# A two-layer graph network: 64 of the rows that an iteration of the second layer gathers are fetched one by one by the sync engine

## The reference

```
edge_index = stack([src, dst])
h = maximum(layernorm(x), 0)
x = x + layer0(h, node_vec1, src, dst, edge_attr_4, edge_attr_64, ...)
h = maximum(layernorm(x), 0)
x = x + layer1(h, edge_attr_4, W1..W5, Ws, Wv, edge_index)

# layer1
s, v = x[:, :64], x[:, 64:].reshape(n, 32, 3)
ss, vv = s[src], v[src]                       # one row of 160 per edge
...                                            # products with the 4 edge numbers and W1..W5
m_agg = segment_sum(m, dst, num_segments=n)
return x + relu(linear(m_agg))
```

## Time and profile before

| what | us |
|---|---|
| median of 3 runs (2083.0 to 2085.46) | 2085.17 |
| the profiled execution | 2084.44 |
| its span, first to last instruction | 2082.6 |
| first layer's edge loop, about | 55 to 1035 |
| second layer's edge loop, about | 1083 to 2070 |
| busy in the span: PE / DVE / POOL / ACT | 1714.7 / 1276.2 / 1467.8 / 172.3 |

### The profile page before, as it was taken

The page is one execution under the profiler, slowest core; times in us unless marked ns, Lnnn a source line. Parts: engine busy times, 40 slices in busy tenths (PEclk is TensorE's granted clock), DMA queues, the critical chain, the costliest instruction groups (busy, mean ns, idle before and its releaser), DMA issues. The chain is left out here.

```text
span 2082.6 us, 41902 instructions
## 1 busy us (share of the span) xinstructions
PE 1714.7 (82%) x15596; PEld 1466.5 (70%) x15596; DVE 1276.2 (61%) x2725; ACT 172.3 (8%) x391; POOL 1467.8 (70%) x1559
## 2 busy tenths in 40 slices
PE   6889899989899898999737878787878787878786
PEld 4666676767666676767527878787878787878776
DVE  5777878787878787787763444444444444444444
ACT  4100000001010101000140000000000000000000
POOL 1777777777777777777457777777777777777772
PEclk9999999999999999999859898988989898989898
DMA  6333334333333333333212222222222222222222
GB/s 210 105 97 98 99 96 109 90 105 98 99 97 99 97 98 99 97 102 97 69 53 71 68 71 71 68 70 69 67 66 66 67 66 66 66 66 67 67 67 65
DMA packets 106120, 176.80 MB, mean 85 GB/s; under 512 B 27328, under 2 KB 73104, under 8 KB 105952
## 3 DMA queue, kind: packets, MB, share of 16 engines
q0 software_dynamic: 73200, 125.03, 24.5%
q1 hardware_dynamic: 30560, 49.88, 7.3%
q10 hardware_dynamic: 2320, 1.44, 0.2%
HBM read 170.10 MB, written 6.14 MB: 85 GB/s over the span
## 5 line engine op out<-in xcount | busy, mean ns | idle before, releaser
L578 POOL DMA_INDIRECT g<-node_table,src x1525 | 1443.6, 947 | 531.2 <-issue 494.8
L836 PE MATMUL w_ps<-H,work 128*128 128x160 f32 x2900 | 486.8, 337 | 196.8 <-DVE work L666 196.8
L836 PEld LDWEIGHTS w_ps<-H,work 128*128 128x128 f32 x2900 | 473.2, 220 | 209.8 <-DVE work L666 209.8
L718 DVE STREAM_TRANSPOSE turned<-sums 128x160 f32<-128x160 f32 x232 | 79.8, 344 | 511.5 <-PE sums L825 464.3
L699 DVE TENSOR_TENSOR work<-w_ps,g 128x384 f32<-128x384 f32 (+3 forms) x693 | 298.9, 459 | 113.5 <-DMA g<-node_table,src 64.3
L790 PE MATMUL w_ps<-fc_sb,work 64*128 64x224 f32 x1612 | 242.1, 399 | 89.1 <-DVE work L693 87.0
L821 PEld LDWEIGHTS sums<-work,sel 128*32 128x32 f32 x6448 | 203.6, 114 | 117.3 <-issue 79.7
L790 PEld LDWEIGHTS w_ps<-fc_sb,work 64*128 64x128 f32 x1612 | 173.4, 200 | 138.8 <-DVE work L693 120.7
L649 DVE TENSOR_TENSOR sel<-mixed,sh 128x896 f32<-128x896 f32 x232 | 251.7, 1085 | 28.9
L821 PE MATMUL sums<-work,sel 128*32 128x160 f32 x6448 | 256.2, 312 | 0.7 <-DVE work L693 0.7
L825 PE MATMUL sums<-g,sel 128*128 128x160 f32 x1612 | 232.7, 302 | 10.4 <-DMA g<-node_table,src 9.8
(11 more groups left out here) (78 smaller groups left out, 495.8 us busy)
## 6 DMA issues: line engine op xcount, KB each, us to landing
feat<-edge_feat_dram SPq DMA_DIRECT2D x60, 512.0 KB
g<-node_table,src POOLq DMA_INDIRECT x1525, 2.6
named<-src_rows_dram SPq DMA_DIRECT2D x30, 128.0 KB, 3.0
X<-x_dram SPq DMA_DIRECT2D x5, 400.0 KB, 6.9
node_table<-H SPq DMA_DIRECT2D x5, 400.0 KB, 2.7
named<-src_rows_dram SPq DMA_DIRECT2D x30, 64.0 KB
sh<-edge_sh_dram SPq DMA_DIRECT2D x1, 1624.0 KB, 8.7
out_dram<-X SPq DMA_DIRECT2D x4, 240.0 KB, 3.3
```

The lines of the kernel that those rows point to most:

```text
L578: nc.gpsimd.indirect_dma_start(out=g[:, u, j, :], out_offset=None, in_=table[layer], in_offset=bass.IndirectOffsetOnAxis(ap=src[:, at:at + ...
L836: last = nc.tensor.matmul(found_at[:, i, 0:D], match[layer][:, i, t, :], H[:, t, :], start=(t == 0), stop=(t == NT - 1))
```

## The change

In the second layer the last tile of group 1 (`ROW_AT = (1, 6)`) is split. POOL gathers its first 64 rows with one indirect DMA, as before but shorter. Rows 64 to 127 are fetched by SP: the 64 node numbers of an iteration are loaded into one partition (`by_row`), read into SP registers eight at a time with bounds 0 to 3124, and each starts a DMA of one row of 640 bytes into one partition of `g`. PE waits for all 64 (`row_landed`) ahead of the last tile of that group. SP's work of an iteration is: wait for the slot, 32 rows, the load of `named` as before with its wait on `named_read`, 32 rows, the load of the next `by_row`.

```diff
+BY_ROW = 64
+ROW_AT = (1, TILES - 1)
+AT_ONCE = 8
...
+            def load_by_row(sp, it):
+                sp.dma_start(by_row[:], src_by_row[bass.ds(it, 1), :]).then_inc(by_row_in, 16)
+
+            def fetch_rows(sp, a, b):
+
+                u, j = ROW_AT
+                for c in range(a, b, AT_ONCE):
+                    _, nodes = nc.values_load_multi_w_load_instructions(by_row[0:1, c:c + AT_ONCE], engines=(mybir.EngineType.SP,),
+                                                                        min_val=0, max_val=N - 1)
+                    for k, node in enumerate(nodes, P - BY_ROW + c):
+                        sp.dma_start(g[k:k + 1, u, j, :], table[layer][bass.ds(node, 1), :]).then_inc(row_landed, 16)
+
+            def sync_turn(sp, f, it, first, last):
+                if not first:
+                    free = sp.snap(UNROLL * f + (ROW_AT[0] + 1 - UNROLL))
+                    sp.wait_ge(agg_done, free)
+                sp.wait_ge(by_row_in, sp.snap(16 * f + 16))
+                sp.sem_inc(pass_left, 1)
+                fetch_rows(sp, 0, BY_ROW // 2)
+                if last:
+                    last_rows(sp, f)
+                else:
+                    more_rows(sp, f, it)
+                fetch_rows(sp, BY_ROW // 2, BY_ROW)
+                load_by_row(sp, 0 if last else sp.snap(it + 1))
+
             def sync_picks(sp):
                 load_named(sp, layer, 0)
+                load_by_row(sp, 0)
                 with passes(sp) as q:
-                    with sp.Fori(0, ITERS - 1) as it:
-                        more_rows(sp, sp.snap(q + it), it)
+                    sp.wait_ge(rows1_out, 16 * len(parts))
+                    sp.sem_inc(pass_left, 1)
+                    sync_turn(sp, q, 0, True, False)
+                    with sp.Fori(1, ITERS - 1) as it:
+                        sync_turn(sp, sp.snap(q + it), it, False, False)
                     f = sp.snap(q + (ITERS - 1))
-                    last_rows(sp, f)
+                    sync_turn(sp, f, ITERS - 1, False, True)
                     pass_over(sp, q)
                     end = sp.snap(16 * f + 32)
                     sp.wait_ge(named_in[layer], end)
+                    sp.wait_ge(by_row_in, end)
                     sp.sem_inc(pass_left, 1)
...
                     for j in range(tiles):
                         at = TILES * (UNROLL * it + u) + j
+                        n = P - BY_ROW if not own_weights and (u, j) == ROW_AT else P
                         nc.gpsimd.indirect_dma_start(
-                            out=g[:, u, j, :], out_offset=None, in_=table[layer],
-                            in_offset=bass.IndirectOffsetOnAxis(ap=src[:, at:at + 1], axis=0),
+                            out=g[0:n, u, j, :], out_offset=None, in_=table[layer],
+                            in_offset=bass.IndirectOffsetOnAxis(ap=src[0:n, at:at + 1], axis=0),
                         ).then_inc(gathered[u], 16 * (1 if j < tiles - 1 else by_pool[u] - tiles + 1))
...
                     for j in range(n):
+                        if not own_weights and (o % UNROLL, j) == ROW_AT:
+                            pe.wait_ge(row_landed, 16 * BY_ROW * f + 16 * BY_ROW * (o // UNROLL + 1))
                         if not own_weights and j == by_pool[o % UNROLL]:
```

More of the change, by code:

```diff
@@ L82, with build @@
 PICKED = ((2,), (0, 2))
-def build(nc, x, node_vec, src_idx, src_rows0, src_rows1, node_id, dst_idx, edge_sh, edge_feat, ident, iota, lin_sc, lin_sc_scale,
+BY_ROW = 64
+ROW_AT = (1, TILES - 1)
+AT_ONCE = 8
+def build(nc, x, node_vec, src_idx, src_rows0, src_rows1, src_by_row, node_id, dst_idx, edge_sh, edge_feat, ident, iota, lin_sc, lin_sc_scale,
           fc1, fc2, big0, big0_scale, l1_pair, l1_pair_scale, l1_out, l1_out_scale, out):
@@ L128, in build @@
         node_id_sb = sb("node_id_sb", [P, NT])
+        by_row = sb("by_row", [1, BY_ROW], I32)
         named = sb("named", [P, max(map(len, PICKED)), P], I32)
@@ L178, in build @@
         named_in = [sem(f"named_in{l}") for l in range(2)]
+        by_row_in = sem("by_row_in")
         big0_in = sem("big0_in")
@@ L474, in edge_layer @@
             named_read = sem(L + "named_read")
+            row_landed = sem(L + "row_landed")
             match_done = sem(L + "match_done")
@@ L1199 @@
         "src_rows1": picked_rows(1),
+        "src_by_row": np.ascontiguousarray(e_src.reshape(ITERS, UNROLL, TILES, P)[:, ROW_AT[0], ROW_AT[1], P - BY_ROW:]),
         "node_id": np.arange(NPAD, dtype=np.float32).reshape(NT, P).T.copy(),
```

## The result

| | before | after |
|---|---|---|
| median of the runs, us | 2085.22 (2083.0 to 2085.46) | 2673.45 (2670.31 to 2673.86) |
| span of the profiled execution, us | 2082.6 | 2668.4 |

The changed kernel takes 1.282 times as long, 95% interval 1.280 to 1.284. The prediction was 2605 us (2270 to 3165), slower with a chance of 0.96.

What follows compares the result with a forecast made beforehand. The chain of waits between DVE and PE was taken as the bound, 34.1 us per iteration. SP's turn of 51.8 us adds 491 us over 28 periods, iteration 0 adds 30: 2084.4 + 521 = 2605 us, range 2270 to 3165.

Steps and rivals of the forecast that it cites:

- POOL's relief: POOL's gather of 64 rows, 0.6 us shorter: nothing in the steady loop, -1.2 us at the start, hidden under the loss.
- The rival of 2067 us: POOL secretly the bound, so 29 x 0.6 = 17 us come back; a gain beyond 0.2% had 1%.
- What one row costs: SP's price t per row: address, DMA instruction, check, share of the read and gaps, 0.75 us in sum.
- the 3035 rival: Every value pays its own register read on SP: t = 0.98, period 66.5, 3035 us; dear reads had 19%.
- SP's turn: Second limit: 64 rows, two loads and the landing of `by_row`, 64 t + 3.8 = 51.8 us, setting the period; 48%.
- the first limit: The 32 rows behind DVE's copy stall PE's seventh tile by 32 t - 9.1 us, period 49.0; binding alone had 25%.
- the fixed part: The 3.8 us of SP's turn besides its 64 rows: loads of `named` and `by_row`, and the landing of `by_row`.
- the landing of `by_row`: SP waits at the head of the next turn for the numbers to arrive, 3.0 us by the nearest row.
- iteration 0: The second layer's first iteration: rows there at 1135 where PE took that tile at 1105.2, +30 us.
- t = 0.5: Case of the second half alone binding: stall 6.9 us, +193, iteration 0 about 10, 2285 us, the range's low end.
- t = 0.66: Row price at which the two limits are equal; the forecast time there was given as 2455 us.
- a wholly slow find: PE's later find all at half clock if the first limit alone binds: at most +2.9 us per iteration.

Runs made afterwards that it cites:

- compare_first: The kernel before, with DVE's copy and compare of a picked tile put ahead of select in the second layer: 2049.40 us, ratio 0.982 to the kernel before.
- rows32_front: The changed kernel with 32 rows instead of 64, all fetched ahead of the load of `named`: 2085.72 us, ratio 1.0002 to the kernel before.
- rows32_back: The changed kernel with 32 rows instead of 64, all fetched behind the load of `named`: 2479.04 us, ratio 1.189 to the kernel before.
- rows64_front: The changed kernel with all 64 rows fetched ahead of the load of `named`: 2682.44 us, ratio 1.286 to the kernel before.
- rows_unchecked: The changed kernel without the bounds check of the 64 values: 2267.87 us, ratio 1.087 to the kernel before.
- numbers_early: The changed kernel with `by_row` in two halves, each reloaded as soon as it is read: 2687.84 us, ratio 1.288 to the kernel before.
- compare_first_half: compare_first with the last tile of group 1 gathered for 64 rows only, SP fetching none and PE waiting for none: 2047.13 us, ratio 0.981 to the kernel before.
- rows_static: The changed kernel with its 64 row DMAs from fixed rows, without read, check or address arithmetic: 2082.67 us, ratio 0.9995 to the kernel before.

## Why the prediction was right

**The bound before, and POOL's relief.** Right that DVE and PE set the period: compare_first, which shortens their chain and takes nothing from POOL, brought the period from 34.1 to 32.4. (rows32_front can't tell, since it hardly relieves POOL.) POOL was close behind, though: 32.4 is its own 26 gathers. The relief itself was mis-sized: I took 0.6 us for half a gather, it is 0.05. It entered the sum as -1.2 hidden under a loss, so it did no harm there, but it would have misled anyone who counted on 29 x 0.6 = 17 us. The rival of 2067 us is out by the same 0.05.

**What one row costs.** Forecast 0.75, measured 0.77. The register read was 0.10 rather than 0.07, the check 0.165 rather than 0.196, the address 0.066 rather than 0.083, the DMA instruction 0.224 where I took 0.25 (a one-partition DMA is cheaper to issue than the 0.333 of the earlier trace rows), the gaps 0.21 rather than 0.15. That eight values share one read was the step on which the 3035 rival hung, and it was right.

The Trainium skill's 200 ns for each register in bulk (Runtime: NRT & Kernel Launch, Instruction fetch mechanics) would have given 1.6 us for eight, an estimate. For registers read from on-chip memory this trace has 0.775, and the measurement decides.

**Which limit binds.** Both limits held as mechanisms, each shown alone: the second half behind DVE's copy by rows32_back against rows32_front, SP's turn by rows64_front against the changed kernel, the change from one to the other by rows_unchecked. The landing that I put into the first limit was too long: 2.6, taken from the gather, against 1.2 (the last row's DMA is issued at 1725.53, PE goes on at 1726.76). It lay on the limit that doesn't bind in the changed kernel.

**SP's turn.** Forecast 64 x 0.75 + 3.8 = 51.8, measured 54.05. Of the 2.25 that are missing, 64 x 0.019 = 1.2 is the row, the rest the fixed part, 4.9 instead of 3.8. One step in it failed by its mechanism: I put 3.0 us there for the landing of `by_row`. SP waited for `by_row` once, 0.8 us. numbers_early loads them half a turn sooner and gains nothing. What stands in that place is the pause of 2.4 us at the loop's back edge, behind which the numbers land unseen, with three more of 0.35; about these I had written nothing. The two loads with the head of the turn make up the remaining 1.5 of the 4.9, where I had 0.8. That the fixed part came out near is luck. The trace of before could hint at it only through the length of the new body, 8 + 64 x 5 = 328 instructions for SP and a few more, where there were a few.

The Trainium skill has the rule that my forecast lacked (Runtime: NRT & Kernel Launch, Instruction fetch mechanics): a taken branch whose target isn't in the instruction memory's current window forces a fetch before execution goes on. The packets of the instruction queue, 162 against 29, agree. How long a body has to be for it, the runs only put between about 200 and about 330 instructions.

**The sum.** 28 x (54.05 - 34.25) = 554, and iteration 0, whose last row was issued at about 1131.5 and landed 1.2 later, 27.5 after PE's old 1105.2: +582, measured +585.8 in the span. Forecast +521. Of the 61 between 521 and 582, 28 x 2.25 = 63 is SP's turn, and iteration 0 gives 2.5 back.

Two of the forecast's side sums are a little off, and neither touches 2605. At t = 0.5, iteration 0 adds 1084 + 32 + 3 - 1105.2 = 14 us, not 10. At t = 0.66 its formula gives 2439 us, not 2455.

**TensorE's clock.** PE idles more and its mean granted clock in the steady loop fell from 0.90 (1180 to 2070 us) to 0.75 (1300 to 2600 us). While SP sets the period, no loss from it shows, as forecast. Under the first limit I had feared up to 2.9 us per iteration from a wholly slow find. It didn't come: in rows32_back the long find takes 8.9 us on average, against 9.96 before.

## What to carry to other kernels

An idle engine isn't free capacity until the price of one piece on it is multiplied out against the period: 64 x 0.77 = 49 us didn't fit into 34, and 32 x 0.77 = 25 us did. Where a wait stands in the middle of an in-order queue, what comes behind it has only the time between that wait and its reader, so put first what is needed first and waits for least (rows32_front against rows32_back, 393 us). And before relieving an engine, see whether it is the bound and whether the relief changes the number of its instructions; here swapping two calls on the chain that bound gave 1.8%, and relief for POOL nothing.

## What the runs showed of the hardware that was not expected

- An indirect DMA on POOL costs 1.25 us of POOL for 128 rows and 1.20 for 64 (the changed kernel; 1.26 and 1.21 in compare_first_half): at these sizes the price is nearly all for the instruction.
- Issuing a DMA of one row into one partition costs SP 0.224 us at a register address, one of 128 partitions 0.333. The bounds check of its index costs as much: 0.165 and two gaps of 0.045, and a row costs 0.25 less without it (0.77 against 0.52, rows_unchecked).
- 64 such DMAs per iteration, 1856 in all, disturbed nothing else (rows_static, ratio 0.9995).
- A loop body of about 330 instructions on SP paid 2.4 us at each back edge and three pauses of 0.35 on its way; one of about 200 paid 0.3 at the branch (rows_unchecked).
